# Cross-attention and a top-2 expert layer: the routing scatters whole normalised rows instead of an eight-byte table entry

## The reference

```python
x = x + softmax(q(ln0(x)) @ k(ctx).T / sqrt(256)) @ v(ctx)
h = ln0(x)                                   # the "normalised rows"
top-2 of h @ Wr.T + br ; w = softmax of the two logits
out = sum over the two experts e of  w_e * (gelu(h @ W1[e].T + b1[e]) @ W2[e].T + b2[e])
x = x + layernorm(out + h, eps=1e-12) * ln_w + ln_b
```

## Time and profile before

| | us |
|---|---|
| median of 3 runs | 691.11 (688.15 to 692.05) |
| span of the profiled execution | 699.0 |

### The profile page before, as it was taken

How to read it: one execution, slowest core, us unless ns; L and a number is a source line. 1 busy time by engine, 2 the same in 40 slices (tenths; PEclk the granted TensorE clock), 3 DMA queues, 4 the chain that set the end, 5 groups by cost and what they waited for, 6 DMA issues and landing times.

```text
span 699.0 us, 18311 instructions
## 1 busy us (share of the span) xinstructions
PE 611.3 (87%) x5018; PEld 519.9 (74%) x5019; DVE 402.7 (58%) x1201; ACT 298.9 (43%) x717; POOL 316.7 (45%) x536
## 2 busy tenths in 40 slices
PE   5998888878648999999999999999999999953775
PEld 4998777777536889989899898998989887631232
DVE  1587766776564546455464554645546454428785
ACT  2687656665233333333423334333343333315452
POOL 3125655666643233434345343453434433216775
PEclk8899999998558999999999999999999999995555
DMA  7456656546423111111111111111111111028712
GB/s 227 134 167 110 157 149 145 118 128 164 82 79 114 34 41 53 51 39 60 38 53 53 38 60 45 45 53 38 60 38 53 46 39 40 24 87 257 251 60 90
DMA packets 53731, 61.48 MB, mean 88 GB/s; under 512 B 12840, under 2 KB 46976, under 8 KB 53568
## 3 DMA queue, kind: packets, MB, share of 16 engines
q1 hardware_dynamic: 40480, 38.16, 20.2%
q0 software_dynamic: 8864, 18.69, 8.5%
q10 hardware_dynamic: 4352, 4.20, 1.8%
HBM read 42.98 MB, written 18.04 MB: 87 GB/s over the span
## 4 chain that ended last, share of the span: by engine, by line
PE 62%; DMA 10%; POOL 8%; issue 8%; DVE 5%; ACT 2%; SPq 2%; another core or an unknown queue 2%; DVEq 1%; POOLq 1%; ACTq 0%
PE bank L842 10%; PE bank L844 9%; PE bank L843 9%; PE bank L864 9%; PE bank L866 9%; PE bank L865 9%; DMA w2lo<-expert_rows 4%; POOL slot_table L575 3%; PE bank L821 2%; DMA x<-in_x_dram 2%; POOL rn L547 1%; DMA stage<-in_L_ffn_W_dram 1%; DVE st L1142 1%; POOL w1lo L648 1%
## 5 line engine op out<-in xcount | busy, mean ns | idle before, releaser
L1021 ACT ACTIVATE stage<-bank,b1s 128x256 f32<-128x256 f32 (+1 forms) x312 | 124.7, 451 | 190.6 <-PE bank L844 186.2
L842 PE MATMUL bank<-xnt,w1hi 128*128 128x256 f16 (+1 forms) x624 | 164.8, 266 | 6.9 <-issue 3.5
L843 PE MATMUL bank<-xnt,w1hi 128*128 128x256 f16 (+1 forms) x624 | 164.0, 265 | 0.0
L844 PE MATMUL bank<-xnt,w1lo 128*128 128x256 f16 (+1 forms) x624 | 164.0, 265 | 0.0
L606 POOL DMA_INDIRECT expert_rows<-xn,sidx x71 | 70.7, 996 | 195.7 <-DVE xn L1290 183.5
L1280 DVE CAST stage<-stage 128x512 f16<-128x512 f32 (+1 forms) x156 | 62.7, 402 | 164.8 <-PE bank L866 161.2
L864 PE MATMUL bank<-w2hi,stage 128*128 x568 | 154.9, 273 | 2.1 <-DVE xn L1290 1.8
L865 PE MATMUL bank<-w2lo,stage 128*128 x568 | 154.8, 273 | 0.0
L866 PE MATMUL bank<-w2hi,stage 128*128 x568 | 154.8, 273 | 0.0
L1282 DVE TENSOR_TENSOR stage<-stage 128x512 f16<-128x512 f32 (+1 forms) x156 | 100.7, 645 | 5.4
L592 POOL DMA_INDIRECT xn<-tokens_dram,gidx x71 | 70.6, 995 | 43.3 <-issue 34.5
(11 more groups left out here) (180 smaller groups left out, 922.9 us busy)
## 6 DMA issues: line engine op xcount, KB each, us to landing
stage<-in_L_ffn_W_dram SPq DMA_DIRECT2D x16, 768.0 KB
x<-in_x_dram SPq DMA_DIRECT2D x16, 256.0 KB
tokens_dram<-xn SPq DMA_DIRECT2D x16, 256.0 KB
stage<-in_L_ffn_W_dram SPq DMA_DIRECT2D x16, 256.0 KB
w1hi<-expert_rows SPq DMA_DIRECT2D x16, 256.0 KB, 3.3
w2lo<-expert_rows SPq DMA_DIRECT2D x16, 256.0 KB, 4.0
out_dram<-w1lo ACTq DMA_DIRECT2D x16, 256.0 KB, 2.2
ctx_sb<-in_ctx_dram SPq DMA_DIRECT2D x16, 120.0 KB
```

Source lines behind the costliest of these rows:

```text
L842: nc.tensor.matmul(dst, w1hi[:, col], xhi[:, k, 0:bt], start=(k == 0), stop=False)
L843: nc.tensor.matmul(dst, w1hi[:, col], xlo[:, k, 0:bt], start=False, stop=False)
L844: ins = nc.tensor.matmul(dst, w1lo[:, col], xhi[:, k, 0:bt], start=False, stop=(k == KD - 1))
L1021: ins = nc.scalar.activation(h32[:, c * bt:(c + 1) * bt], f_h[q][:, (c % 2) * bt:(c % 2 + 1) * bt], ACT.Gelu, bias=b1s[p][:, c:c + 1], sca ...
```

## The change

The normalised rows are kept in three buffers `xr` of 272 floats a row: 256 values, the token's number, the number of its first expert, padding. Publishing scatters these rows (1088 bytes each) straight to slot order in DRAM (`slot_rows`). So `slot_table`, its blank fill, `tokens_dram` and its 16 stores, the 39 loads of slot entries, the 71 gathers and the copies of indices go. A block's rows are one plain load of SP. Where a result row goes is worked out per block by three small operations of DVE (`aim`) from the row's own token and expert number; rows beyond an expert's count get a number out of bounds, and the scatter of results skips them. So that such rows hold finite numbers, SP writes eight pads (seven of 128 rows, one of 512) behind the last used slot of each expert, as soon as the counts are known. `load_late(3)` moves behind the pads. The loop over steps 8 to 15 is written out. ACT's wait before `xn2` is now for the scatters of the batch three before, POOL waits for `xn2` before it scatters, and `mt`, `bv_bc` and `ident_c` move into spare columns of `stage` (so `load_late(0)` and `load_late(1)` wait for their last readers).

The place and the number of the scatters stay; a copy became an iota, and the source is the row itself. The core of the diff:

```diff
 # sync: routing step
-            sp.wait_ge(consts_pool, 1)
-            for i in range(PADS):
-                sp.dma_start(table_v[...], pad_rows[i]...).then_inc(table_blank, 16)
...
+                if t == NB:
+                    sp.wait_ge(k_mm, NB)
+                if t == NB + 1:
+                    sp.wait_ge(v_ready, NB)
                 if isinstance(t, int) and t in (NB, NB + 1, NB + 3):
                     load_late((NB, NB + 1, NB + 3).index(t))
-                if route is not None:
-                    sp.wait_ge(xn2_ready, r + 1)
-                    sp.dma_start(tok_v[...], xn2[pr][:, :, :]).then_inc(xn2_stored[pr], 16)
 # sync: transition
-            load_late(3)
             sp.wait_ge(ctxt_mm, NB)
             sp.dma_start(lnb_bc[:, :], ln_b.partition_broadcast(P)).then_inc(shift_loaded, 16)
+            sp.wait_ge(x1_ready, NB)
+            sp.wait_ge(pad_known, 1)
+            for e in range(E):
+                n = SPARE if e == E - 1 else 1
+                r = sp.value_load(pad_row[0:1, e:e + 1], min_val=0, max_val=(UNITS - n) * P)
+                sp.dma_start(slot_rows[bass.ds(r, n * P), :]..., x1...[:, 0:n * ROW]).then_inc(padded, 16)
+            load_late(3)
+            sp.wait_ge(padded, 16 * E)
 # gpsimd: publish
-                    nc.gpsimd.tensor_copy(rows_now[p][:, :, :], ids[:, bass.ds(b * n, n), :]).then_inc(rows_copied, 1)
+                    nc.gpsimd.iota(xr[b % XR][:, :, AT_TOKEN], [[P, TJ]], base=b * SQ, ...).then_inc(token_noted, 1)
+                    pool.wait_ge(xn2_ready, b + 1)
                     alone(pool, slots_ready, b + 1, tally_pool)
                     for a in range(n):
                         nc.gpsimd.indirect_dma_start(
-                            out=slot_table, ... in_=rows_now[p][:, a, :], ...).then_inc(published[p], 16)
+                            out=slot_rows, ... in_=xr[b % XR][:, a // TOPK, :], ...).then_inc(published[b % XR], 16)
 # gpsimd: experts (fetch became aim, its gathers are gone)
-                for t in range(tb):
-                    nc.gpsimd.indirect_dma_start(out=xg[p][:, t, :], out_offset=None, in_=tokens_dram, ...)
+                pool.wait_ge(targets_ready, j + 1)          # in give
 # scalar
-            act.wait_ge(table_blank, 16 * PADS)
-                    at_least(act, x2t_mm, n - 1)
-                    at_least(act, xn2_stored[ps], 16 * ms)
-                    normalised(xn2[ps], n, u, 1, xn2_ready)
+                    at_least(act, published[n % XR], ROUTED * (n // XR))
+                    normalised(xn2[n % XR], n, u, 1, xn2_ready)
 # tensor
-                pe.wait_ge(gathered[p], landed(m + 1))
+                pe.wait_ge(rows_in[p], 16 * (m + 1))
 # vector: publish, route, counts
-                    at_least(dve, published[pk], ROUTED * mk)
+                    nc.vector.tensor_copy(xr[r % XR][:, :, AT_EXPERT:AT_EXPERT + 1], ix[:, :, 0:1])
+            nc.vector.tensor_copy(cntf, bank[5][:, 0:E])
+            nc.vector.tensor_tensor(pad_row, bank[5][0:1, 0:E], slot0[0:1, :], ALU.add).then_inc(pad_known, 1)
...
+            ... eleven operations behind blocks_ready that end in left_out ...
 # vector: experts, three small operations a block
+                    nc.vector.tensor_scalar(second_choice, xg[AT_EXPERT], eidf[j], TOK, ALU.not_equal, ALU.mult)
+                    nc.vector.tensor_tensor(target, second_choice, xg[AT_TOKEN], ALU.add)
+                    nc.vector.tensor_tensor(targets[j], target, left_out[j], ALU.max).then_inc(targets_ready, 1)
```

More of the change, by code:

```diff
@@ L141, in build @@
         xn = [sb(f"xn{i}", [P, TJ, D]) for i in range(2)]
-        xn2 = [sb(f"xn2_{i}", [P, TJ, D]) for i in range(2)]
+        XR = 3
+        xr = [sb(f"xr{i}", [P, TJ, ROW]) for i in range(XR)]
+        xn2 = [xr[i][:, :, 0:D] for i in range(XR)]
         xnt = sb("xnt", [P, KD, SQ])
@@ L172, in build @@
         slotf = sb("slotf", [P, TJ * TOPK])
-        slots = [sb(f"slots{i}", [P, TJ * TOPK], I32) for i in range(2)]
-        rows_now = [sb(f"rows_now{i}", [P, TJ * TOPK, 2], I32) for i in range(2)]
+        slots = sb("slots", [P, NB, TJ * TOPK], I32)
         vals = sb("vals", [P, NB, TJ, TOPK])
@@ L294, in build @@
         seen_ready = sem("seen_ready")
-        rows_copied = sem("rows_copied")
-        published = sem2("published")
+        token_noted = sem("token_noted")
+        published = [sem(f"published{i}") for i in range(XR)]
         w_mm = sem("w_mm")
@@ L378, in one @@
                 step(2 * m + u, u, *back)
[L379 to L384, removed]
+            for t in range(NB + last):
                 one(t // 2, t % 2)
@@ L455, in _ @@
             steps(sp, step, 4)
-            load_late(3)
             sp.wait_ge(ctxt_mm, NB)
             sp.dma_start(lnb_bc[:, :], ln_b.partition_broadcast(P)).then_inc(shift_loaded, 16)
-            for p in range(2):
-                sp.wait_ge(published[p], ROUTED * NB // 2)
+            sp.wait_ge(x1_ready, NB)
[3 more added lines that the diff above has]
+                r = sp.value_load(pad_row[0:1, e:e + 1], min_val=0, max_val=(UNITS - n) * P)
+                sp.dma_start(slot_rows[bass.ds(r, n * P), :].rearrange("(p j) c -> p (j c)", j=n),
+                             x1[:, :, :, :].rearrange("p b j d -> p (b j d)")[:, 0:n * ROW]).then_inc(padded, 16)
+            load_late(3)
+            sp.wait_ge(padded, 16 * E)
+            for i in range(XR):
+                sp.wait_ge(published[i], ROUTED * len(range(i, NB, XR)))
             sp.wait_ge(blocks_ready, 1)
@@ L511, in _ @@
         def _(pool):
-            for i in range(PADS):
-                nc.gpsimd.iota(pad_rows[i][:, :, 0], [[1, P]], base=0, channel_multiplier=0)
-                ins = nc.gpsimd.iota(pad_rows[i][:, :, 1], [[1, P]], base=TOPK * TOK + i * P * P, channel_multiplier=P)
-            ins.then_inc(consts_pool, 1)
             nc.gpsimd.memset(ident[:, :], 0.0)
@@ L520, in _ @@
             nc.gpsimd.memset(seen[:, :], 0.0)
+            for i in range(XR):
+                nc.gpsimd.memset(xr[i][:, :, D:], 0.0)
             nc.gpsimd.memset(minus_half[:, :, :], -0.5).then_inc(pool_self, 1)
@@ L1314, in _ @@
             x_low(0, 1)
+            for p in range(2):
+                for part in range(3):
+                    aim(0, p, part)
             split(0, 0)
```

186 lines of the change are left out of this document (106 added, 80 removed).

## The result

The changed kernel takes 683.61 us (median of 4 runs, 682.3 to 684.52) against 690.77 (4 runs, 688.15 to 692.05, three of them those of the section on the time before) for the kernel before: a ratio of 0.9922, 95% interval 0.9895 to 0.9949. That is 7.2 us, where 1.8 were forecast. So there are two questions: where the 7 us came from here, and where they are there.

A forecast was written before the change was run, and what follows sets the result against it. It took TensorE's matmuls to bound the experts and POOL's scatter burst to pace the routing. Terms -1.7 - 0.8 + 1.0 - 0.3 = -1.8 took the median of 691.1 to 689.3 us, range 677 to 698.

The forecast's parts named there:

- A: Routing steps: POOL's burst of scatters sets the pace as before, small gain, 686 to 692 us, likeliest 689.3; chance 0.45.
- B: Routing steps: late signals go with SP's loads between scatters, POOL's 1.99 us of standing shrink; 679 us (672 to 683); chance 0.25.
- The rows that bind the routing: Routing step of 10.37 us: norm, scatters, late signal, aggregate; paced by POOL's burst, not by TensorE.
- Stores of normalised rows: SP's traffic in routing: 16 stores leave, 64 scatters of 139 KB come; the larger traffic fits the step, 0 us.
- Scatters by the row: POOL's 64 scatters in routing: 1088-byte rows cost at most 0.04 us apiece over 8-byte entries; taken as 0.
- Loop written out: Routing steps 8 to 15: first scatter starts 0.21 us sooner behind the norm in eight steps, -1.7 us.
- Blank fill: Start of the kernel: ACT's first normalised batch no longer waits 1.23 us for the fill, -0.8 us (0 to -1.2).
- ACT's new wait: ACT in routing: the wait for scatters of three batches before is over when ACT comes to it, 0 us.
- Transition: Last scatter to first expert matmul: slot entries and gather go, late weights stand behind pads; +1.0 us (-0.4 to +3).
- Experts: Expert blocks: gathers leave POOL, VectorE's added operations hide under TensorE, second and third block turn sooner; -0.3 us (-1 to +1).
- C: Transition: late weights behind the pads come 4 us later, +5 instead of +1, 694 to 698 us; chance 0.18.
- D: Routing: scatters land over 5.6 us after the burst, so ACT waits every step; +10, 700 to 702 us; chance 0.12.

The follow-up runs named there:

- e1: Changed kernel, with SP waiting again in each step for ACT's normalised rows before it issues the next weights, no store; 685.76 us, 1.0012 of before.
- e5: Kernel before the change, unchanged, profiled once more; 683.1 us.
- e9: Kernel before, with a bounds check that no row exceeds on the scatters of result rows; 685.48 us, 0.9992 of before.
- e4: Kernel before, with routing steps 8 to 15 written out and nothing else; 684.38 us, 0.9987 of before.
- e3: Kernel before, with SP storing a batch's normalised rows one step later, ahead of the x load; 680.47 us, 0.9934 of before.
- e6: Changed kernel, unchanged, run again on a second chip; 683.46 us, 1.001 of before.
- e11: Changed kernel, unchanged, run a third time on another chip; 684.8 us, 0.9985 of before.
- e8: Changed kernel, with the last load of late weights ahead of the pads; 681.12 us, 0.9979 of before.
- e12: Changed kernel, with 71 unread indirect loads added on POOL, one behind each scatter of result rows; 683.11 us, 0.9988 of before.
- e2: Changed kernel, with SP's wait for ACT's normalised rows and a 256 KB store of them that nobody reads; 692.35 us, 1.0086 of before.
- e10: Changed kernel, with late weights ahead of pads, token numbers written first, skipped rows sent to a dump area without a check; 680.79 us, 0.9959 of before.

## Why the prediction was right, and where not

The time lies in the stated range, but not for the reason that was forecast, and that is luck. It is outside A's own 686 to 692, and by the prediction's own sign ("the forecast is wrong if the steps change by more than 0.3 us") the forecast failed: the steps went from 10.37 to 8.40 us. The range held because it reached into B, whose signs (steps of 9.5 us or less, POOL idle for less than 1 us) came true.

*The rows that bind the routing.* Right in the order (norm, scatters, signal, aggregate), wrong in the cause. The step that failed is the reading of the earlier trace rows as a property of the kernel, "while POOL issues its scatters, and SP its loads between them, other engines' signals come late". POOL scatters as before and loads stand among the scatters in e1, and no signal is late; above all, the same kernel ran without late signals in a later execution (e5). B's bound on the gain was wrong too: it took TensorE's busy time as a floor that leaves 1.45 us a step, and the step fell by 1.97. That busy time went from 8.9 us a step (42.96 of 50) to 8.2 (39.05 of 40). So A, the likeliest case, kept a wait that in this comparison went away, and B came true for another reason than the one it named. The result of 683.6 lies between A's 689.3 and B's 679: nearly all of the 1.99 us a step went, in the profile (17.9 us), of which the times show 7.2 in all.

*Stores of normalised rows, 0:* too little, and not only because of the late signals. Where no signal is late, the scatters' stretch of the kernel before is 129.0 to 131.2 us (e5, e9, e4), with single steps in which the weights, issued behind the store, land after 8 to 10 us. In e3, where the store leaves one step later, it is 125.8, 3 to 4 us less than in e5 and e9, and in the changed kernel 124.4 to 125.0.

*Scatters by the row:* 0.04 us apiece were bounded, 0 was taken. POOL's 64 scatters are 997 ns on average on the page after, 994 before. Right.

*Loop written out, -1.7:* steps are 0.2 to 0.3 us shorter in e4, as priced; its time doesn't resolve it. In the changed kernel POOL has no idle time left in the middle, and the step is 3.40 us from norm to first scatter and 4.92 of burst.

*Blank fill, -0.8:* right. 54.4 to 53.6 between the profiles of the result, but 53.9 against 55.9 and 56.0 in e5, e6 and e11. What moves the start by 2 us there is ScalarE's wait for TensorE's first products, ahead of the first normalised batch (timeline of ScalarE, e6 and e8, the changed form in both):

```profile
15.20 0.16 ACT L920 COPY wv_ext<-bank 128x2 f32<-128x2 f32 x1 [3.56 <-PE bank L690]
```

```profile
12.90 0.16 ACT L920 COPY wv_ext<-bank 128x2 f32<-128x2 f32 x1 [1.46 <-PE bank L690]
```

It is 3.56 us in four executions (e4, e6, e11, e12) and 1.35 to 1.57 in the other ten; eight of TensorE's matmuls ahead of it (L683) took 354 ns each in e6 and 253 in e8, and why is not shown. In the other ten the first normalised batch starts at 14.1 to 14.5 us in the old form, after 0.4 to 1.2 us of waiting for the fill, and at 13.1 to 13.9 in the new, without a wait: 0.8 us sooner on average.

*ACT's new wait, 0:* right for the pace, and close. In the changed kernel ACT waits 0.2 to 0.5 us once in the middle and 2.6 to 3.4 us once in the tail (profiles of after, e6, e11, e12), and in after and e6 the chain doesn't pass through that wait; in e1 it waits six times, and in e2 the landing takes 7.79 us. The prediction's estimate from the Trainium skill, page "DMA: Bandwidth & Descriptors", section on the anatomy of one DMA, was 3.3 us for four scatters that overlap, by a fit that the page gives per DMA. Here, with loads beside them, the scatters of the changed kernel landed 2.4 to 6.1 us after their issue (median 4.0), and the one of e2 after more than twice the estimate; the measurement decides.

*Transition, +1.0 between -0.4 and +3:* 0 between the profiles of the result, +2.0 to +2.5 where the kernel before wasn't disturbed (13.3 to 15.3 and 15.8). The mechanism was right, the weights behind the pads, and e8 gives 1.6 us of it back. The pads took 1.15 us, not 1.24, and the weights' landing 4.29, not 3. VectorE's new operations behind the counts were let delay nothing, but once the weights come first they stand on the chain for 2.7 us (e10, 177.05 to 179.78), ahead of the eviction of late weights.

*Experts, -0.3:* -1.2 between the profiles of the result; 407.1 to 407.8 us in the five profiles of the old form, 405.2 to 407.3 in the nine of the new.

*What the sum left out:* POOL's closing drain, +3.5 us at the end, which in the trace of before costs nothing.

Where the kernel before was not disturbed, the stretches show why the two kernels are level. From e5 to e6 they are +2.0 at the start (TensorE's first products, not the change), -4.0 in the scatters, +2.0 in the transition, -1.8 in the experts and +3.5 at the end, +1.7 together; the spans differ by 1.5, as the entries are rounded. C, the rival on the slower side, had the right place there, though 2 us and not 5, and D's wait came in e1 and e2.

What stays open is why TensorE's signals were late in the profile of before. In that execution transfers were slower as well: the last scatter landed in 6.41 us instead of 4.27. That speaks for something that slowed its traffic, on that chip or at that hour, but it is an argument: the hold was not reproduced, and no run varied it. Nor is it settled whether the signal came late or the rank itself, as the profile models the ends of matmuls.

## What to carry to other kernels

Profile a kernel twice, at two times and on two chips, before a wait that a trace shows in every step is taken for its own: here a wait of 2 us in each step was one execution's. A store that is issued where it must first wait makes the loads behind it late (9.1 and 10.0 us to landing in e5 and e4), and moving it one step later gave 0.9934 of the kernel before (0.9907 to 0.9962), the lowest ratio of the later comparisons, which were made on four chips. When work leaves an engine, look at the program's end too: here a drain that had been hidden now stands alone for 3.4 us.

## What the runs showed of the hardware

POOL's closing drain took 4.18 to 4.19 us in all profiles with 206 indirect transfers, 71 of them loads, and 7.86 us in all with 135 and no such load, whatever the rows and the checks (fourteen profiles). A bounds check that no row exceeds cost nothing measurable (0.9992, interval 0.9963 to 1.0022). An indirect write of 128 rows of 1088 bytes took POOL 997 ns, one of 8 bytes 994.
